# First layer of eight expert MLPs by seven block products instead of eight (Strassen), with the expert stage rebuilt in quarters

## What is computed

```
leaf = product over 3 depths of sigmoid(x @ rw.T + rb) or 1 - sigmoid(...)       # (1250, 8)
h = einsum('nd,edh->neh', x, w1) + b1      # x (1250, 512), w1 (8, 512, 2048)
h = gelu(h)
y = einsum('neh,ehd->ned', h, w2) + b2     # w2 (8, 2048, 512)
out = einsum('ned,ne->nd', y, leaf)
```

## Time and profile before

| | us |
|---|---|
| median of 3 runs (2437.89 to 2440.28) | 2439.18 |
| the profiled execution, its own time | 2441.33 |
| its span, first to last instruction | 2439.5 |
| start of the tree stage's first hidden product | 666.2 |
| last product of the tree stage | 2424.6 |
| TensorE busy in the span | 2287.1 (94%) |
| VectorE, ScalarE, GpSimd busy | 1020.3, 692.6, 326.8 |

### The profile page before, as it was taken

One profiled execution on the slowest core, in us unless ns is written; L12 is line 12 of the kernel. 1 busy time (PEld: TensorE's weight loads), 2 busy tenths in 40 slices (PEclk: granted clock), 3 DMA queues, 4 the chain that ended last, 5 costly groups with the idle time before them and its releaser, 6 DMA issues.

```text
span 2439.5 us, 33802 instructions
## 1 busy us (share of the span) xinstructions
PE 2287.1 (94%) x13459; PEld 2212.7 (91%) x13459; DVE 1020.3 (42%) x1676; ACT 692.6 (28%) x1200; POOL 326.8 (13%) x314
## 2 busy tenths in 40 slices
PE   3998995479999999999999999999999999999998
PEld 3887993449899999999999999999999999999997
DVE  7994447435534242424234242424334242424332
ACT  1335232335332222222222222222222222222221
POOL 1553001110011011011011011011011011111010
PEclk9998997699999999999999999999999999999998
DMA  2000202150121120202011020202011020202101
GB/s 67 3 2 1 70 1 95 61 172 18 35 81 35 35 80 1 70 1 80 18 52 59 22 69 1 80 1 69 29 52 53 18 80 1 69 4 76 35 1 42
DMA packets 73350, 106.03 MB, mean 43 GB/s; under 512 B 7219, under 2 KB 42499, under 8 KB 73211
## 3 DMA queue, kind: packets, MB, share of 16 engines
q1 hardware_dynamic: 68471, 99.87, 12.1%
q0 software_dynamic: 4480, 3.64, 0.5%
q10 hardware_dynamic: 260, 0.51, 0.1%
HBM read 95.08 MB, written 10.40 MB: 43 GB/s over the span
## 4 chain that ended last, share of the span: by engine, by line
PE 73%; DVE 0%; DMA 0%; issue 0%; ACT 0%; POOL 0%; POOLq 0%; SPq 0%; DVEq 0%
PE psum L513 24%; PE psum L515 24%; PE psum L514 24%; PE psum L1552 0%; DMA w_raw<-in_w 0%; PE psum L1819 0%; DVE f_xT_lo L1715 0%; DVE w_lo L1636 0%; ACT f_xT_hi L1768 0%; PE psum L1841 0%; POOL acc L1748 0%; POOLq L1578 0%; ACT f_rows L507 0%; DVE w_hi L1621 0%; DVE x_rows L1708 0%
## 5 line engine op out<-in xcount | busy, mean ns | idle before, releaser
L1670 DVE TENSOR_TENSOR hidden_lo<-gelu,hidden_hi 128x416 fp32r<-128x416 f32 (+1 forms) x384 | 248.0, 646 | 1109.9 <-ACT hidden_hi L1789 1109.2
L1784 ACT ACTIVATE gelu<-psum,b1cols 128x416 f32<-128x416 f32 (+1 forms) x384 | 234.2, 610 | 1286.8 <-PE psum L515 1286.8
L513 PE MATMUL psum<-f_xT_hi,w_hi 128*128 128x416 f32 (+1 forms) x1536 | 542.1, 353 | 0.0
L513 PE MATMUL psum<-hidden_hi,w_hi 128*128 128x416 f32 (+1 forms) x1536 | 541.2, 352 | 0.2 <-DVE hidden_lo L1670 0.2
L514 PE MATMUL psum<-f_xT_lo,w_hi 128*128 128x416 f32 (+1 forms) x1536 | 540.6, 352 | 0.0
L515 PE MATMUL psum<-hidden_hi,w_lo 128*128 128x416 f32 (+1 forms) x1536 | 540.6, 352 | 0.0
L515 PE MATMUL psum<-f_xT_hi,w_lo 128*128 128x416 f32 (+1 forms) x1536 | 540.0, 352 | 0.0
L514 PE MATMUL psum<-hidden_lo,w_hi 128*128 128x416 f32 (+1 forms) x1536 | 538.1, 350 | 0.0
L1748 POOL TENSOR_TENSOR acc<-acc,y_scaled 128x418 f32<-128x418 f32 (+1 forms) x190 | 197.3, 1072 | 1525.4 <-DVE y_scaled L1661 1525.4
L515 PEld LDWEIGHTS psum<-f_xT_hi,w_lo 128*128 128x128 f32 x1536 | 289.4, 188 | 4.6
L514 PEld LDWEIGHTS psum<-hidden_lo,w_hi 128*128 128x128 f32 x1536 | 288.8, 188 | 4.0
(11 more groups left out here) (308 smaller groups left out, 1961.1 us busy)
## 6 DMA issues: line engine op xcount, KB each, us to landing
w_raw<-in_w SPq DMA_DIRECT2D x128, 512.0 KB, 4.3
expert_raw<-in_experts SPq DMA_DIRECT2D x8, 1024.0 KB, 6.6
leaf_all<-leaf_rows SPq DMA_DIRECT2D x8, 625.0 KB, 3.8
rows_by_place_d<-zero_rows SPq DMA_DIRECT2D x1, 2560.0 KB, 15.6
rows_by_place<-rows_by_place_d SPq DMA_DIRECT2D x5, 512.0 KB, 6.6
expert_results_d<-expert_results SPq DMA_DIRECT2D x16, 160.0 KB, 5.4
x_rows<-in_x SPq DMA_DIRECT2D x1, 2500.0 KB
W_raw<-in_gnn_W SPq DMA_DIRECT2D x4, 512.0 KB, 4.1
```

The lines of the kernel that those rows point to most:

```text
L513: t.matmul(out, stat[0], mov[0], start=start, stop=False)
L1670: v.tensor_tensor(hlo[:, s % 4, 0:w], G[:, s % 3, 0:w], hhi[:, s % 4, 0:w].bitcast(F32), ALU.subtract).then_inc(lo_cut, 1)
L1784: a.activation(G[:, s % 3, 0:w], g.psum[:, first_bank(n), 0:w], ACT.Gelu, bias=g.b1cols[:, e * 16 + half * 8 + 2 * q + j:e * 16 + half * 8 ...
```

## The change

Three things go together.

**Seven products for eight.** For a pair (256 hidden columns, called a group G; there are 64) and token blocks 0 and 1 (416 each), w1's 512 x 256 part is cut in 2 x 2 blocks of 256 x 128 and x in 2 x 2 blocks of 256 x 416. Seven half products (each two slices of the contraction, six matmuls) of sums of blocks replace eight. Token block 2 (418) is computed as before (`product_2`).

- The sums of x (T1 to T4) are made once, by VectorE and GpSimd, and cut into high and low, before the steady part.
- The four sums of w1 are made for each group by GpSimd (`weight_sums`), cast by ScalarE (`s_high`), and their low part is made by VectorE (`s_rest`).
- The results are put together by VectorE in five operations with one PSUM and one SBUF input (`sum_2`, `sum_3`, `hidden_22`, `hidden_21`, `hidden_12`), after ScalarE has moved the first product out of PSUM (`move_p1`); gelu of the three mixed ones then reads SBUF.

**Quarters.** The second layer is accumulated over 512 hidden columns instead of 1024, so 96 drains of four operations instead of 48 (and the bias factor is 1/4).

**Rings of two pairs.** `raw1` and `raw2` have one buffer each, the cut weights two pairs each, and the ring of hidden tiles has three entries (before four). Loops over experts are unrolled on all engines. The tree nodes' logits are plain fp32 matmuls with 7 stationary columns on a transposed fp32 copy of x (`xf`), no longer cut in high and low; `x_rows` transposes go to `xf` by ScalarE alone.

In the loop of TensorE below, `product2` waits for `move_p1`, `product7` for `sum_2`, `product3` for `hidden_22`, `product_2(G, 0)` for the gelu of the group's first tile and `product_2(G, 1)` for `sum_3`. `slot(G, i)` is `second(Q, 0, i)` in an odd group and `second(Q - 1, 2, 2 + i)` in an even one: a quarter Q is an even and an odd group. In the lead-in, `logits`, `turn` and group 0 stand woven together ahead of this loop.

The diff, cut to its core:

```diff
+TBLOCKS = [(0, 416), (416, 832), (832, 1250)]
+HRING = 3
...
         @block.gpsimd
         def _(q):
+            def weight_sums(n):
+
+                a11, a12 = raw1[:, 0:2, 0:128], raw1[:, 2:4, 0:128]
+                a21, a22 = raw1[:, 0:2, 128:256], raw1[:, 2:4, 128:256]
+                s1, s2, s3, s4 = (g.ssum[n % 2][:, i] for i in range(4))
+                q.wait_ge(w1_in, 16 * (n + 1))
+                if n >= 2:
+                    q.wait_ge(product, made(n - 2, P3))
+                q.tensor_tensor(s1, a21, a22, ALU.add).then_inc(s_sum, 1)
+                q.tensor_tensor(s3, a11, a21, ALU.subtract).then_inc(s_sum, 1)
+                q.wait_ge(s_sum, 4 * n + 1)
+                q.tensor_tensor(s2, s1, a11, ALU.subtract).then_inc(s_sum, 1)
+                q.wait_ge(s_sum, 4 * n + 3)
+                q.tensor_tensor(s4, a12, s2, ALU.subtract).then_inc(s_sum, 1)
...
+            for G in range(GROUPS):
+                Q = G // 2
+                if G and G + 1 < GROUPS:
+                    weight_sums(G + 1)
+                if G % 2 == 0 and Q:
+                    add_blocks(Q - 1, 2, range(KD))
+                if G % 2:
+                    add_blocks(Q, 0, range(KD))
+                    add_blocks(Q, 1, range(KD))
...
         @block.scalar
         def _(a):
...
+            for G in range(GROUPS):
+                Q, m = G // 2, 2 * (G % 2)
+                move_p1(G)
+                if G + 1 < GROUPS:
+                    s_high(G + 1)
...
+                gelu_11(G)
+                high(Q, 0, m)
+                gelu_mixed(G, C22, 1, 1)
+                gelu_mixed(G, C21, 0, 1)
+                high(Q, 0, m + 1)
+                gelu_mixed(G, C12, 1, 0)
...
+                gelu_2(G, 0)
+                gelu_2(G, 1)
...
+                if G % 2:
+                    for b in (1, 2):
+                        for k in range(4):
+                            high(Q, b, k)
...
         @block.tensor
         def _(t):
...
+            def half_product(bank, stat, which, start, stop):
+
+                for k in range(2):
+                    ins = cut_products(t, g.psum[:, bank, 0:TBW], (stat[0][:, k, :], stat[1][:, k, :]),
+                                       (g.xchi[:, which, k, :], g.xclo[:, which, k, :]), start and k == 0,
+                                       stop and k == 1, again=not start)
...
+            for G in range(1, GROUPS):
+                product1(G)
+                product5(G)
+                product6(G)
+                product2(G)
...
+                slot(G, 0)
+                product7(G)
+                product4(G)
+                slot(G, 1)
+                product3(G)
+                product_2(G, 0)
+                product_2(G, 1)
+                if G % 2:
+                    second(Q, 0, 2)
+                    second(Q, 0, 3)
+                    for m in range(4):
+                        second(Q, 1, m)
+                    second(Q, 2, 0)
...
+                    second(Q, 2, 1)
...
+        @block.vector
+        def _(v):
...
+            for G in range(GROUPS):
+                Q, m = G // 2, G % 2 * 2
+                if G + 1 < GROUPS:
+                    w1_cut(G + 1)
+                sum_2(G)
+                if G + 1 < GROUPS:
+                    w1_rest(G + 1)
+                low(Q, 0, m)
+                sum_3(G)
+                hidden_22(G)
+                hidden_21(G)
+                if G + 1 < GROUPS:
+                    s_rest(G + 1)
+                low(Q, 0, m + 1)
+                hidden_12(G)
+                if G % 2 == 0 and Q:
+                    drain(Q - 1, 2)
+                w2_cut(G)
+                if G % 2:
+                    low(Q, 1, 0)
+                    drain(Q, 0)
+                    for k in (1, 2, 3):
+                        low(Q, 1, k)
+                    low(Q, 2, 0)
+                    drain(Q, 1)
...
```

More of the change, by code:

```diff
@@ L1454, with tree_buffers @@
 STEPS = 48
[L1457 to L1461 removed]
+def tree_buffers(nc, g, low, middle, high):
+    room = Room(nc, low)
+    g.xchi = room("x_sums_hi", [128, 7, 2, TBW], F32R)
+    sums_at = room.next
+    g.xclo = room("x_sums_lo", [128, 7, 2, TBW], F32R)
+    g.xcsum = Room(nc, sums_at)("x_sums", [128, 7, 2, TBW], F32)
@@ new lines, in weights, with sums, product1, product5 @@
+            def weights(G, i, j):
+                c = slice(i * 128, (i + 1) * 128)
+                return w1hi[:, G % 2, 2 * j:2 * j + 2, c], w1lo[:, G % 2, 2 * j:2 * j + 2, c]
+            def sums(G, i):
+                return g.shi[G % 2][:, i], g.slo[G % 2][:, i]
+            def product1(G):
+                t.wait_ge(w1_lo, G + 1)
+                if G:
+                    t.wait_ge(active, 6 * (G - 1) + 5)
+                half_product(BANK_A, weights(G, 0, 0), X11, True, True)
+            def product5(G):
+                t.wait_ge(s_lo, G + 1)
+                if G:
+                    t.wait_ge(mixed, summed(G - 1, C12))
+                half_product(BANK_E, sums(G, 0), T1, True, True)
@@ new lines, in product6, with product2, product7, product4 @@
+            def product6(G):
+                if G:
+                    t.wait_ge(active, 6 * (G - 1) + 6)
+                half_product(BANK_B, sums(G, 1), T2, True, True)
+            def product2(G):
+                t.wait_ge(p1_moved, G + 1)
+                half_product(BANK_A, weights(G, 0, 1), X21, False, True)
+            def product7(G):
+                t.wait_ge(mixed, summed(G, U2))
+                half_product(BANK_B, sums(G, 2), T3, False, True)
+            def product4(G):
+                half_product(BANK_F, weights(G, 1, 1), T4, True, True)
@@ L1858, in first @@
-                ins.then_inc(hidden, 1)
-            def second(e, s):
-                half, b, q, j = where(s)
-                w = BLOCKS[b][1] - BLOCKS[b][0]
-                if b == 0 and j == 0:
-                    t.wait_ge(cut, e * PAIRS + half * 4 + q + 3)
-                t.wait_ge(lo_cut, e * STEPS + s + 4)
+                    ins = cut_products(t, g.psum[:, BANK_B if j else BANK_A, 0:BW],
+                                       (w1hi[:, G % 2, k, c], w1lo[:, G % 2, k, c]),
+                                       (g.x2hi[:, k, :], g.x2lo[:, k, :]), k == 0, k == KD - 1)
@@ L1867, in second @@
+                ins.then_inc(product, 1)
+            def second(Q, b, m):
+                n, w = tile_no(Q, b, m), width(b)
+                if b == 0 and m % 2 == 0:
+                    t.wait_ge(w2_lo, 2 * Q + m // 2 + 1)
+                t.wait_ge(lo_cut, n + 1)
                 for d in range(KD):
-                    if s % 8 == 0:
-                        t.wait_ge(y_free, e * 24 + 4 * (s // 8) + d + 1)
+                    if m == 0 and n:
+                        t.wait_ge(y_free, 4 * (3 * Q + b - 1) + d + 1)
@@ L1889, in _ @@
             turn(8)
-            t.wait_ge(x_lo, 8)
-            first(0, 0)
+            t.wait_ge(x_lo, 1)
+            product1(0)
             turn(9)
+            t.wait_ge(added, NT)
             node_turn(0)
-            t.wait_ge(x_lo, 9)
-            first(0, 1)
-            t.wait_ge(added, 9)
+            t.wait_ge(x_lo, 2)
+            t.wait_ge(moved, 8)
+            product5(0)
             logits(2)
             node_turn(1)
-            first(0, 2)
+            t.wait_ge(x_lo, 3)
@@ L1915, in _ @@
-            for s in range(STEPS):
-                second(LAST, s)
-                if s + 2 < STEPS:
-                    first(LAST, s + 2)
-                if s + 1 in OUT_AT:
-                    i = OUT_AT.index(s + 1)
-                    if i % 3 == 0:
-                        t.wait_ge(acc_done, 4 + 24 * LAST + (16 if i == 0 else 20))
-                    turn_out(t, i)
-            t.wait_ge(acc_done, 4 + 24 * LAST + 22)
+            product2(0)
+            t.wait_ge(x_lo, 5)
+            product7(0)
@@ L1925, in _ @@
+            second(LASTQ, 2, 2)
+            t.wait_ge(acc_done, 12 * LASTQ + 8)
+            for i in range(3, 6):
+                turn_out(t, i)
+            second(LASTQ, 2, 3)
+            t.wait_ge(acc_done, 12 * LASTQ + 10)
             t.wait_ge(last_acc, 2)
```

679 lines of the change are left out of this document (403 added, 276 removed).

## The result

The changed kernel takes 2382.52 us in the median (2382.28 to 2384.3 in four runs) beside 2439.37 for the kernel before on the same chip: 0.977 of its time (95% interval 0.975 to 0.979), 57 us less. The forecast was 2384, so the number is hit within 1.5 us. The chain of reasons behind it is not: a wait put at 11 us did not come, the distance of the products cost 5.2 us more and the lead-in 3.5 us more than forecast. These errors nearly cancel, so that the number is that close is luck.

The account below looks back on a forecast made before the run. TensorE, busy for 94% of the span, was taken as the bound: 73.0 us saved by 384 fewer matmuls, less 6.8 for lead-in, transposes and restarts, gives 2373.3; plus 11 of odd-group waits, span 2384.3, median 2384. Range 2367 to 2414 us.

Parts of the forecast that it names:

- The saving: TensorE over all 64 pairs: 384 matmuls fewer at 0.190 us each, 73.0 us saved.
- The lead-in: Before the steady part: product3 of group 0 starts at 683.5, group 0 ends at 690.3; with transposes and restarts costs 6.8 us.
- Logits: Tree nodes' logits: 36 matmuls of 6.8 us become 12 plain fp32 ones, at most 4.7 us, about 1.4 per block.
- The wait in the odd groups: TensorE before product3: chain over GpSimd's w1 sums ends at 28.8, due 28.5; 0.35 us in 31 odd groups, 11 us.
- TensorE stays full: Steady part: port turns cost less or GpSimd ends 1 us earlier; 2373 us, or 2368 with smoother lead-in; chance 0.27.
- the forecast: Steady part: TensorE waits 0.15 to 0.8 us in odd groups, total 2377 to 2398 us; chance 0.42.
- The distance: TensorE's products: the time from one matmul to the next stays at 0.190 us, since length, stationary size and form stay.
- The term for met waits: TensorE's waits already met, some 10 more per group: taken as 0, with 13 us as upper end.
- The tail: Behind the last product (drains, last transposes, stores): as before, 14.9 us.
- Sums of 0.87: GpSimd's w1 sums take 0.87 us each or more: 1.1 us more per odd group, 2416 us; chance 0.23.
- Slower: Same odd-group chain over 2.1 us late, w1 sums near 1.06 each, product3 waits 3 us: 2466 us; chance 0.05.
- The signs: In the trace: odd-group product3 waits of 0.3 us, none at product7, sums near 0.6; against: even-group waits, another distance, load waits.

Follow-up runs that it names:

- Experiment 1: Changed kernel with product4 issued twice in every group, putting the saved 384 matmuls back: 2454.40 us, 1.0057 of the kernel before.
- Experiment 9: Changed kernel with VectorE's node_logits(0) ahead of the first sum of x instead of behind the third: 2381.94 us, 0.9758 of the kernel before.
- Experiments 4: Changed kernel with one extra GpSimd operation per group ahead of the four w1 sums, result overwritten: 2390.93 us, 0.9797 of the kernel before.
- experiment 5: Changed kernel with two extra GpSimd operations per group ahead of the w1 sums, the second waiting for the first: 2414.11 us, 0.989 of the kernel before.
- Experiments 2: Changed kernel with the four waits for a drained bank at each token block's start merged into two: 2382.69 us, 0.9763 of the kernel before.
- 3: Kernel before with 1344 more waits on TensorE, all met, ahead of every three second-layer matmuls: 2440.15 us, 1.0001 of the kernel before.
- 7: Kernel before with 84 unused VectorE additions of 512 elements per expert: 2454.34 us, 1.0056 of the kernel before.
- 8: Kernel before with eight unused GpSimd additions of 512 elements after each adding of a drained block: 2461.71 us, 1.0087 of the kernel before.
- 10: Changed kernel with the rings of hidden tiles and the cut w2 at each other's place in SBUF: 2386.42 us, 0.9776 of the kernel before.
- experiment 12: Changed kernel with hidden-tile rings, block 2's x and the cut w2 padded to start on multiples of 64 bytes: 2377.51 us, 0.9744 of the kernel before.

## Why the prediction was right, and where it was not

**The saving (right).** 384 matmuls at 0.190 were put at 73.0. Experiment 1 gives 71.9, with the rest of the change held.

**The lead-in (3.5 us too short; the hit to 1 us is luck).** Group 1 was put at 690.3 and starts at 691.30. But the forecast counts on the times of the profiled execution before, in which the projection's first matmul starts at 627.23 and not at 624.71. From there the forecast is 63.1 us and the measured time 66.6. The step that failed is "with `node_logits(0)` between them TensorE gets to `product5(0)` at 671.6": it starts at 671.65, but in a stage that began 2.5 us earlier and behind a wait of 2.48 for that drain, which the steps did not have. At the lower clock that follows, `product5` takes 2.2 us and `logits(2)` 3.67, so the drain of those logits, and with it everything behind it in VectorE's queue, comes later than forecast: `product3` starts at 684.50 for 683.5. Experiment 9 gets 2.0 of these 3.5 us back by the place of the drain.

**Logits (size wrong, without consequence).** "About 1.4 per block" was summed and "1.57 for four" the upper end; 2.97 us are recorded, two instructions for each matmul. The earlier trace rows had four instructions, which are two such matmuls. Together 9.6 us instead of 4.7, beside 6.8 for what they replace; most of it lies where TensorE would wait for the next tile anyway.

**The wait in the odd groups (wrong: 11 us forecast, none there).** The step that failed is the last of the chain, "P3 was due at 28.5. With a restart the wait is 0.35 us in each of 31 odd groups". The chain ends at 28.1, not 28.8. (The terms written there add up to 28.7: 24.3, 1.06, 1.82, 1.35 and 0.15. That would have made the wait 0.2 us, 7 in all.) Where the 0.7 are:
- 0.3: the sums are done at t = 24.0, not 24.3. The step "adds end at 20.0, cast at 20.6" held GpSimd's first sum behind VectorE's w1 cast. In the rows it went ahead (1535.47, t = 19.6), within the turn-taking. This outweighs that a sum takes 0.73 and not 0.60.
- 0.1: gelu starts before the recorded end of `s_high` (1540.85 and 1540.94).
- 0.2: `sum_3` and `hidden_22` are 0.58 and 0.59 and follow closely, 1.13 from the end of the low part to their end, where 1.35 was taken. A general 0.65 for VectorE's small operations was right for a sum of work and too long for a chain.
- The rest is that sum, 0.1.

So it is 0.45 us early where it was forecast 0.35 late, an error of 0.8 in a chain of 28. Experiments 4 and 5 show the same chain at the same place once GpSimd has 0.75 or 1.5 us more. So the rival "TensorE stays full" (chance 0.27) had the mechanism, and the forecast (0.42) had it wrong.

**The distance (wrong: 0.190 taken, 0.1906 measured, 5.2 us).** The step is "I take 0.190", with form and length unchanged as the reason. 8766 products took 1670.8 us where 1665.5 was summed. Most of the growth is in the six long distances per quarter. Experiments 2 and 3 rule out the cost of met waits, 7 and 8 the load of VectorE and GpSimd; 10 and 12 show that the place of buffers in SBUF changes them, 2 that the instructions ahead have a small part. How they do it is open. The term for met waits ("I take 0, upper end 13 us") was right: 1344 of them gave 1.0001.

**The tail (0.9 short).** 14.9 was taken; from 2364.65 to the end of the span it is 15.8.

**The sum.** Forecast span 2384.3; less 11 for the wait, plus 5.2 for the distance, 3.5 for the lead-in and 0.9 for the tail, less 2.5 for the earlier start of this execution's stage gives 2380.4, the measured span. On the median, which does not have that early start: 2384 - 11 + 5.2 + 3.5 + 0.9 = 2382.6, for 2382.52. The full-TensorE rival's 2373.3 plus the last four terms gives the same span. With the padding of experiment 12 the span is 2375.7, near that rival.

**The other rivals.** Sums of 0.87 (0.23): undisturbed they are 0.73, and more GpSimd time was made in experiment 5: 1.5 us more gave 2414, where the rival wanted 1.1 us for 2416. Its chain was right, its start 0.8 us off. Slower (0.05): it wanted 2.1 us of lateness and the chain has 0.45 to spare. (Its price was summed too low: sums that are 3.2 us later make the wait 3.5 us and not 3, and the time 2482.) The signs: no wait in even groups, `product7` never waits in the steady part, and the loads never hold VectorE, as said. The wait in odd groups and the sums of 0.6 us are not there, and of what was to be wrong, "a distance of matmuls other than 0.190 where nothing waits" came.

**The pages.** The trace does not agree with the shorter distance, 176 ns, that the prediction worked out from the Trainium skill (TensorE: Matmul & The Clock Gate, section Back-to-back issue gap) for these columns: even with padded buffers it is 190 ns. The prediction left out a condition there: the page gives that formula for a single isolated matmul, and says that in a stream of matmuls with their weight loads it over-counts for many columns, with 131 ns measured at 512. The 190 ns of these fp32r products lie above both. The trace does agree with the exclusive lock of the Trainium skill (SBUF — State Buffer, section SBUF: two separate sides): the sum of 0.73 that meets the w1 rest has 1.72, and it ends 0.59 after that rest does.

## What to carry to other kernels

A chain through three engines whose lateness is estimated at a third of a microsecond can be on time; price it from rows of the very operations with their overlaps, not from a rounded mean, and measure what is to spare by adding one operation and then two. A saving of matmuls comes in full only while the distance stays, so read it by counting matmuls in a stretch without waits. When it has grown by some tenths of a per cent, list the distances by their place in the loop: here six matmuls of 276 had most of the growth, in every round, and another layout of the buffers (here padding to multiples of 64 bytes) took it away. And compare two traces from a point that the change leaves alone: stages ahead of it can differ by 2 us and more from one execution to the next, as much as the effects looked for.

## What the runs showed that was not expected

- The place of buffers in SBUF moves the distance of fp32r matmuls of 416 and 418 columns by 0.6%: 2621, 2626 and 2637 in 500 us for three layouts of the same work. Most of the extra time stands at 7, 6 or none of a quarter's 276 products. The mechanism is open.
- 1344 met semaphore waits more on TensorE: ratio 1.0001. 190 fewer in the changed kernel moved some of the long distances, with all addresses the same, and gave 0.8 us.
- A GpSimd addition of 128 x 256 takes 0.73 us, more than the line from 416 to 2048 elements gives (0.54).
- After 2.48 us of idle time in an otherwise busy stretch the granted clock was 0.56 for 2.2 us and 0.80 for the next 3.7.
